# Recurrent stage of a fused decoder chain: bonus, gather, residual and statistics take other places in the step

## The chip, the cores and the metric

One core of a Trainium2 chip. The metric is the device time of one execution in microseconds: 3461.31 us before, the median of three runs (3460.58 to 3463.86). Below, TensorE is PE in the profile, VectorE DVE, ScalarE ACT, GpSimd POOL and SyncE SP.

## The reference, cut to what matters

Four layers follow one another on 16 sequences of 128 tokens with 512 features, in float32: masked self and cross attention with a feed-forward part (L0), grouped cross attention (L1), a recurrent block (L2) and a latent cross attention with a feed-forward part (L3). The change touches L2 alone:

```python
xa = _ln(x, ln1_w, ln1_b)
sx = concatenate([state[:, 1:2] - xa[:, :1], xa[:, :-1] - xa[:, 1:]], axis=1)
xxx = einsum(tanh((xa + sx * maa_x) @ maa_w1).reshape(b, l, 5, DM), maa_w2)
xm = xa[:, :, None] + sx[:, :, None] * (maa_stack + xxx)          # xk, xw, xv, xr, xg
w = exp(-exp(time_decay + tanh(xw @ td_w1) @ td_w2))
r, k, v, g = xr @ Wr.T, xk @ Wk.T, xv @ Wv.T, silu(xg @ Wg.T)
def step(s, (r_t, k_t, v_t, w_t)):
    a = k_t[..., :, None] * v_t[..., None, :]
    out = einsum('bhi,bhij->bhj', r_t, u * a + s)                  # u * a: the bonus
    return a + w_t[..., :, None] * s, out
og = head_norm(out) * gn_w + gn_b
x1 = x + og * g @ Wo.T
xc = _ln(x1, ln2_w, ln2_b)                                         # and a shift by one token again
return x1 + sigmoid(xr2 @ Wfr.T) * (square(relu(xk2 @ Wfk.T)) @ Wfv.T)
```

There are 32 heads of 16 x 16 states per sequence.

## The kernel before, in words

The program is a row of phases (self, cross, mlp, group, rec, latent, pmlp), with a barrier between two of them. The recurrent phase, `recurrence_phase` from L2159, handles one sequence per step and keeps five in flight. In step n the names stand for these sequences: `ahead` is n+1 (its rows are normalised, transposed and shifted), `front` n (low-rank mixes, decay, v, k, r, g), `middle` n-1 (the recurrence proper), `back` n-2 (head norm, output projection, residual, second norm, ffn keys and half of the receptance rows), `tail` n-3 (the rest of the ffn and the result). `run_steps` (L2142) runs steps -1 to 18, those in the middle in a loop of two steps.

Every engine has its own queue with a fixed order, written out by hand in its own `step` function: SyncE at L2352, GpSimd at L2408, ScalarE at L2566, VectorE at L2763, TensorE at L3042. Engines are tied together by semaphores alone. PSUM has five shared banks (`StepBanks`, L2096): the list at L2229 says in which order the items of a step use each bank, and TensorE's `begin` (L2858) waits for the use before to be free. Beside them, rec_out takes the head sums and two banks hold k.

The recurrence of a sequence is cut into 8 units (four feature chunks by two halves of the head). For unit u VectorE makes k times v (`inputs`, L2668, instruction L2674), then a scan over time (`scan`, L2678, L2686); GpSimd multiplies the states by r (`multiply_states`, L2382, L2386); TensorE sums over the head (`sum_heads`, L2981, L2987). Four buffers S circulate, whose first columns ScalarE copies (`first_states`).

The bonus is r times k on VectorE (`bonus_products`, L2690), a sum over the head weighted by u on TensorE (`bonus`, L2973), a copy to SBUF on ScalarE (`bonus`, L2539) and a product with v on GpSimd (`bonus_values`, L2390). `gather` (L2694) adds it to the head sums. Then comes the head norm: `mean` and `variance` on TensorE (L2991, L2999), `head_centre` and the Newton iterations of `head_rsqrt` on VectorE (L2699, L2704), `squares` and `affine` on ScalarE, `rstd_t` (L3007), `gated` (L2729). `out_rows` (L3012) projects; `residual` (L2735) adds the rows loaded again and takes mean and variance (`norm_stats`, L2625); `rsqrt` on GpSimd (L2375) makes the power -1/2 and its product with the negated mean; `normalise_back` and `shifted_back` on ScalarE (L2478, L2482) and `mix_back` on VectorE (L2745) feed the ffn. `stats_front` and `normalise_front` do the first norm for the sequence ahead.

The mixes (`mix`, L2645) come from TensorE in pairs (`mix_pair`, L2926); decay, v, k, r and g follow. `own_weights.wait` and `setup_done` guard weights and a few constants that VectorE prepares at the phase's start (L2828 to L2851).

## Time and profile before

| | us |
|---|---|
| median of three runs | 3461.31 |
| the profiled execution, its own time | 3457.59 |
| its span | 3455.8 |
| recurrent phase in the trace, about | 1571 to 2455 |

| engine | busy over the span | share |
|---|---|---|
| TensorE, matmul | 3175.1 us | 92% |
| VectorE | 1776.9 us | 51% |
| ScalarE | 1160.8 us | 34% |
| GpSimd | 793.3 us | 23% |

The shares are means over phases with different limits. In the page's slices VectorE is busy nine tenths only in the recurrent phase. A line of the timeline gives start, duration, engine, source line, operation and tiles, then in brackets the idle time just before it and what ended that idle. Neighbouring instructions of one kind are merged, and the printed ends of neighbours overlap by up to a tenth of a microsecond, so differences of starts are the better price.

### The profile page before, as it was taken

How to read it: one execution, taken by the hardware profiler on the slowest of the kernel's cores; microseconds unless marked ns; L12 is line 12 of the kernel's file. 1: busy time of each engine (PE TensorE's matmuls, PEld its weight loads, DVE VectorE, ACT ScalarE, POOL GpSimd, SP SyncE). 2: the span in 40 equal slices, each digit the busy share in tenths (PEclk: the TensorE clock that was granted, in tenths of full speed). 3: DMA queues.
4: the chain of work that ended last, by engine and by line, in shares of the span. 5: the costliest groups of instructions: out<-in, count | busy, mean ns of one | idle time of the engine just before them, and what ended most of it. 6: DMA issues, size and time to landing. Idle time of an engine off the chain costs nothing. (4 is left out here: it accounts for less than half of the span.)

```text
span 3455.8 us, 52394 instructions
## 1 busy us (share of the span) xinstructions
PE 3175.1 (92%) x19136; PEld 2078.5 (60%) x19136; DVE 1776.9 (51%) x2577; ACT 1160.8 (34%) x4083; POOL 793.3 (23%) x565
## 2 busy tenths in 40 slices
PE   7999899989999888886899999997799999899999
PEld 5666566657676655555666666664355555567675
DVE  4655455510000178874899999998254544400000
ACT  2444233421111266661333443342233333311111
POOL 2333233310000012222444444445000000100000
PEclk9999999989999999998899999998999999999999
DMA  4110231110000131112111111110130110101000
GB/s 166 42 46 27 80 131 52 40 64 22 15 21 17 42 150 47 49 39 68 35 51 38 37 49 37 41 43 28 64 133 26 36 41 20 49 22 33 21 33 12
DMA packets 104307, 170.17 MB, mean 49 GB/s; under 512 B 16512, under 2 KB 54016, under 8 KB 100736
## 3 DMA queue, kind: packets, MB, share of 16 engines
q1 hardware_dynamic: 99296, 124.58, 11.4%
q10 hardware_dynamic: 4896, 44.04, 3.1%
q8 instruction: 74, 1.21, 0.1%
q14 instruction: 41, 0.34, 0.0%
HBM read 135.03 MB, written 33.55 MB: 49 GB/s over the span
## 5 line engine op out<-in xcount | busy, mean ns | idle before, releaser
L2386 POOL TENSOR_TENSOR rec_S<-rec_S,rec_r_t 128x1024 f32<-128x1024 f32 x128 | 302.0, 2359 | 362.4 <-DVE rec_S L2686 362.3
L2686 DVE TENSOR_TENSOR_SCAN rec_S<-rec_decay,rec_S 128x1024 f32<-128x1024 f32 x128 | 318.0, 2484 | 5.8 <-ACT rec_S L2446 1.5
L2076 PE MATMUL mlp_bank<-mlp_src_t,region_a 128*128 128x256 f32 x1024 | 224.1, 382 | 3.1 <-ACT mlp_src_t L1997 3.1
L2076 PE MATMUL pmlp_bank<-pmlp_src_t,region_a 128*128 128x256 f32 x1024 | 224.7, 382 | 1.9 <-ACT pmlp_src_t L1997 1.9
L2088 PE MATMUL pmlp_bank<-region_a,pmlp_h_t 128*128 128x512 f32 x512 | 221.1, 593 | 0.0
L2088 PE MATMUL mlp_bank<-region_a,mlp_h_t 128*128 128x512 f32 x512 | 221.1, 593 | 0.0
L2076 PEld LDWEIGHTS mlp_bank<-mlp_src_t,region_a 128*128 128x128 f32 x1024 | 196.2, 192 | 32.9 <-issue 6.8
L2076 PEld LDWEIGHTS pmlp_bank<-pmlp_src_t,region_a 128*128 128x128 f32 x1024 | 196.6, 192 | 31.7 <-issue 5.5
L1505 ACT ACTIVATE group_scores<-group_scores,group_negmax 128x128 f32<-128x128 f32 x512 | 197.6, 392 | 28.4 <-DVE group_negmax L1599 18.5
L2043 DVE TENSOR_TENSOR mlp_y<-mlp_bank,mlp_xres 128x512 f32<-128x512 f32 x16 | 11.1, 692 | 374.2 <-PE mlp_bank L2088 374.2
L2043 DVE TENSOR_TENSOR pmlp_y<-pmlp_bank,pmlp_xres 128x512 f32<-128x512 f32 x16 | 11.1, 692 | 363.5 <-PE pmlp_bank L2088 363.5
L2006 ACT ACTIVATE pmlp_h_t<-pmlp_bank,vectors 128x256 f32<-128x256 f32 x128 | 53.7, 470 | 353.6 <-PE pmlp_bank L2076 353.6
L2006 ACT ACTIVATE mlp_h_t<-mlp_bank,vectors 128x256 f32<-128x256 f32 x128 | 53.6, 470 | 347.9 <-PE mlp_bank L2076 347.9
L2088 PEld LDWEIGHTS mlp_bank<-region_a,mlp_h_t 128*128 128x128 f32 x512 | 97.0, 191 | 118.4 <-issue 118.4
L2088 PEld LDWEIGHTS pmlp_bank<-region_a,pmlp_h_t 128*128 128x128 f32 x512 | 97.0, 190 | 118.4 <-issue 118.4
L2674 DVE TENSOR_TENSOR rec_S<-rec_vb,rec_k 128x1016 f32<-128x1016 f32 x128 | 154.0, 1203 | 0.0
L599 ACT ACTIVATE latent_scores<-latent_scores,region_a 128x256 f32<-128x256 f32 x256 | 126.4, 497 | 71.7 <-DVE region_a L789 71.7
L2987 PE MATMUL rec_rec_out<-rec_S,head_sum 128*32 128x256 f32 x1024 | 84.8, 404 | 45.8 <-POOL rec_S L2386 45.8
L973 PE MATMUL latent_pjA<-latent_src_t,F_query_key 128*128 128x512 f32 x256 | 122.0, 602 | 3.3 <-ACT latent_k_t L589 2.3
L599 ACT ACTIVATE self_scores<-self_scores,self_negmax 128x128 f32<-128x128 f32 x256 | 98.8, 390 | 77.0 <-DVE self_negmax L789 77.0
L599 ACT ACTIVATE cross_scores<-cross_scores,cross_negmax 128x128 f32<-128x128 f32 x256 | 98.7, 390 | 76.4 <-DVE cross_negmax L789 76.4
L1979 POOL TENSOR_TENSOR mlp_xres<-mlp_x,rows 128x512 f32<-128x512 f32 x16 | 20.2, 1264 | 341.0 <-DVE mlp_y L2043 329.6
(366 smaller groups left out, 6495.1 us busy)
## 6 DMA issues: line engine op xcount, KB each, us to landing
rec_vb<-v_by_head SPq DMA_DIRECT2D x32, 512.0 KB, 4.2
region_a<-in_C_w ACTq DMA_DIRECT2D x2, 4096.0 KB, 18.8
region_a<-in_G_w ACTq DMA_DIRECT2D x2, 4096.0 KB, 18.0
self_xres<-in_x SPq DMA_DIRECT2D x16, 256.0 KB, 2.6
rows_A<-self_xres SPq DMA_DIRECT2D x16, 256.0 KB, 2.0
cross_ctx_t<-in_ctx_t SPq DMA_DIRECT2D x16, 256.0 KB, 3.3
cross_xres<-rows_A SPq DMA_DIRECT2D x16, 256.0 KB, 2.6
rows_B<-cross_xres SPq DMA_DIRECT2D x16, 256.0 KB, 2.0
```

What stands on the lines that cost most here:

```text
L599: nc.scalar.activation(S[:, u, at, :], S[:, u, at, :], ACT.Exp, bias=negmax[:, u, at.start // KB:at.start // KB + 1], accum_out=rowsum[:, ...
L973: last = nc.tensor.matmul(pj.bank(item)[:, :], Wk[:, c, n * 128:n * 128 + 128], src_t[:, c, :, :], start=c == 0, stop=c == C - 1)
L1505: nc.scalar.activation(S[:, u, at, :], S[:, u, at, :], ACT.Exp, bias=negmax[:, u, at:at + 1], accum_out=rowsum[:, u // UPS, sum_column(u, ...
L1979: nc.gpsimd.tensor_tensor(xres[:, k, :], xr[:, k, :], row(cfg["b2"]), ALU.add)\
L2006: hidden = nc.scalar.activation(h_t[:, 2 * n + i, :], ph.bank(("h", n))[:, i * TT:(i + 1) * TT], ACT.Gelu_apprx_tanh, bias=vec(cfg["b1"], ...
L2043: nc.vector.tensor_tensor(y[:, k, :], po.bank(("out", k))[:, :], xres[:, k, :], ALU.add)\
L2076: product = nc.tensor.matmul(ph.bank(item)[:, i * TT:(i + 1) * TT], W1[:, c, f:f + 128], src_t[:, c, :, :], start=c == 0, stop=c == C - 1)
L2088: product = nc.tensor.matmul(po.bank(item)[:, :], h_t[:, c, k * T:k * T + T], W2[:, c, :], start=c == 0, stop=c == HC - 1)
L2386: nc.gpsimd.tensor_tensor(S[u % 4][:, :, :], S[u % 4][:, :, :], bcast(r_t[:, s.k, UNITS[u][0], :], [128, JH, T], 1), ALU.mult)\
L2674: nc.vector.tensor_tensor(S[u % 4][:, :, 1:T], vb[jh][:, :, 0:T - 1], bcast(k_bank[s.k][:, m * T:m * T + T - 1], [128, JH, T - 1], 1), ALU ...
L2686: nc.vector.tensor_tensor_scan(St[:, :, :].rearrange(flat), decay[m][:, :, :].rearrange(flat), St[:, :, :].rearrange(flat), 0.0, ALU.mult, ...
L2987: last = nc.tensor.matmul(rec_out[32 * g:32 * g + 32, jh * 2 * T:(jh + 1) * 2 * T], head_sum, S[u % 4][:, 2 * g:2 * g + 2, :], start=m == ...
```

## The change

It moves work to other places in the queues, and separates two buffers. The bonus product of `front` is made at the end of a step, where that of `middle` was made in its middle; the matmuls, the copy and the product with v follow early in the next step. The bonus's bank use moves from bank b to bank n. On VectorE the gather stands ahead of the first mix, the residual ahead of the output and of the inputs of unit 4, the front statistics ahead of unit 5. On TensorE one quarter of the receptance rows goes from the end of a step behind the low-rank product of the next, and the sum of unit 7 behind the low-rank transposes. On ScalarE the front normalisation goes ahead of the backward shifts. The negated mean is taken on GpSimd. x1 has two buffers, the normalised rows xn2 have their own (the squares of the head norm share it), so that of these only the tanh of the receptance waits for the store. In the first step TensorE and ScalarE no longer wait for constants and weights ahead of the first rows, but ahead of the low-rank product.

```diff
-        x1 = sb("x1", [128, D])
+        x1 = sb("x1", [128, SL, D])
-        y = xn2 = sb("y", [128, D])
+        xn2 = sb("xn2", [128, D])
+        sq = xn2[:, :].rearrange("p (c t) -> p c t", c=C)
+        y = sb("y", [128, D])
...
-            ("a", "mx", 0), ("a", "lt", 0), ("b", "mix1", 0), ("a", "mix2", 0), ("n", "mean", 2),
+            ("a", "mx", 0), ("a", "lt", 0), ("b", "mix1", 0), ("a", "mix2", 0), ("n", "c", 1), ("n", "mean", 2),
...
-            ("b", "c", 1), ("b", "x", -1), ("d", "fk", 2),
+            ("b", "x", -1), ("d", "fk", 2),
...
                 pool.wait_ge(var_done, n + 1)
+                nc.gpsimd.tensor_tensor(out[:, 2:3], tile[:, 6:7], minus_one[:, :], ALU.mult)
                 nc.gpsimd.tensor_tensor(out[:, 0:1], tile[:, 9:10], minus_half[:, 0:1], ALU.pow).then_inc(out_done, 1)
                 pool.wait_ge(out_done, n * 2 + 1)
-                nc.gpsimd.tensor_tensor(out[:, 1:2], tile[:, 8:9], out[:, 0:1], ALU.mult).then_inc(out_done, 1)
+                nc.gpsimd.tensor_tensor(out[:, 1:2], out[:, 2:3], out[:, 0:1], ALU.mult).then_inc(out_done, 1)
```

GpSimd's step:

```diff
                     first_columns(back)
                 if middle:
+                    bonus_values(middle)
                     multiply_states(middle, 2)
...
                     multiply_states(middle, 4)
-                if middle:
-                    multiply_states(middle, 5)
                 if ahead and not is_first(ahead.n):
                     rsqrt(ahead.n - 1, stats, rstd, front_norm[2], rstd_done)
                 if middle:
+                    multiply_states(middle, 5)
                     multiply_states(middle, 6)
-                    bonus_values(middle)
```

ScalarE (`rows_front`, `normalise_back`, `sigmoid_tanh` and the step):

```diff
+                if is_first(s.n):
+                    act.wait_ge(setup_done, SETUP)
...
-                wait_count(act, stored, s.n * 16)
-                normalise(s.n, xn2, x1, rstd2, rstd2_done, xn2_done)
+                normalise(s.n, xn2, x1[:, s.k, :], rstd2, rstd2_done, xn2_done)
...
                 full(act, s, "fr")
+                wait_count(act, stored, s.n * 16)
...
                     low_rank_copy(front)
+                if middle:
+                    bonus(middle)
                 if middle:
                     make_decay(middle, 3)
...
                     receptance(front)
+                if ahead and not is_first(ahead.n):
+                    normalise_front(ahead)
                 if back:
                     shifted_back(back)
...
                     make_decay(front, 0)
-                if ahead and not is_first(ahead.n):
-                    normalise_front(ahead)
-                if front:
                     gate(front)
-                if middle:
-                    bonus(middle)
...
-            act.wait_ge(setup_done, SETUP)
             run_steps(act, step)
```

VectorE:

```diff
-                nc.vector.tensor_scalar(tile[:, 8:9], tile[:, 6:7], -1.0, None, ALU.mult)
...
             def bonus_products(s):
                 freed(dve, s, "r")
+                dve.wait_ge(k_full, s.n + 1)
...
-                if not is_first(s.n):
-                    freed(dve, Before(s), "fv")
+                if not (isinstance(s.n, int) and s.n < 2):
+                    freed(dve, Before(s, 2), "fv")
...
                     scan(middle, 0)
+                if back:
+                    gather(back)
                 if front:
                     mix(front, 1)
-                if back:
-                    gather(back)
...
                     mix(front, 3)
+                if back:
+                    residual(back)
                 if tail:
                     output(tail)
                 if middle:
                     inputs(middle, 4)
-                if back:
-                    residual(back)
-                if middle:
                     scan(middle, 4)
                 if front:
                     mix(front, 4)
+                if ahead and not is_first(ahead.n):
+                    stats_front(ahead)
                 if middle:
                     inputs(middle, 5)
                     scan(middle, 5)
-                    bonus_products(middle)
-                if ahead and not is_first(ahead.n):
-                    stats_front(ahead)
-                if middle:
                     inputs(middle, 6)
...
                     shift_front(ahead)
+                if front:
+                    bonus_products(front)
```

TensorE:

```diff
-            own_weights.wait(pe)
-
...
             def low_rank(s):
+                if is_first(s.n):
+                    own_weights.wait(pe)
+                    pe.wait_ge(setup_done, SETUP)
...
                     low_rank(front)
+                if tail:
+                    ffn_gate(tail, 1)
+                if front:
+                    low_rank_t(front)
                 if back:
                     sum_heads(back, NU - 1)
-                if front:
-                    low_rank_t(front)
                 if tail:
                     ffn_gate(tail, 2)
                 if front:
                     mix_pair(front, 1, 2)
+                if middle:
+                    bonus(middle)
...
                     sum_heads(middle, 5)
-                    bonus(middle)
...
-                    ffn_gate(back, 0, 1)
+                    ffn_gate(back, 0)
...
-            pe.wait_ge(setup_done, SETUP)
             run_steps(pe, step)
```

## Rows read from the trace of the kernel before

**Rows 1.** Windows, one steady step: busy (count) PE, PEld, DVE, ACT, POOL; PEclk; DMA; GB/s.

```profile
1961.40:2012.00 50.60, 46.19 (x358) 33.68 (x357) 47.84 (x67) 19.42 (x49) 23.96 (x16) 1.00 0.13 42
```

**Rows 2.** Timeline of VectorE, one steady step from shift to shift.

```profile
1961.43 0.66 DVE L2642 TENSOR_TENSOR rec_sx_t<-rec_xa_t,rec_bank_b 128x512 f32<-128x512 f32 x1
...
1967.10 0.70 DVE L2652 TENSOR_TENSOR rec_bank_b<-rec_bank_b,rec_sx_t 128x512 f32<-128x512 f32 x1 [1.01 <-PE rec_bank_b L2913]
...
2009.01 3.06 DVE L2686 TENSOR_TENSOR_SCAN rec_S<-rec_decay,rec_S 128x1024 f32<-128x1024 f32 x1
...
2012.00 0.66 DVE L2642 TENSOR_TENSOR rec_sx_t<-rec_xa_t,rec_bank_b 128x512 f32<-128x512 f32 x1
```

**Rows 3.** Timeline of VectorE, the same step, units 4 and 5 and around.

```profile
1987.14 0.70 DVE L2652 TENSOR_TENSOR rec_bank_b<-rec_bank_b,rec_sx_t 128x512 f32<-128x512 f32 x1 [0.20 <-PE rec_bank_b L2913]
...
1988.48 0.69 DVE L2758 SCALAR_TENSOR_TENSOR rec_bank_d<-rec_y,rec_bank_d 128x512 f32<-128x512 f32 x1
...
1990.93 0.69 DVE L2740 TENSOR_TENSOR rec_x<-rec_bank_c,rec_xr 128x512 f32<-128x512 f32 x1
...
1992.65 0.15 DVE L2633 TENSOR_SCALAR rec_stats<-rec_stats 128x1 f32<-128x1 f32 x1
...
1992.82 2.29 DVE L2686 TENSOR_TENSOR_SCAN rec_S<-rec_decay,rec_S 128x1024 f32<-128x1024 f32 x1
...
1996.35 1.20 DVE L2674 TENSOR_TENSOR rec_S<-rec_vb,rec_k 128x1016 f32<-128x1016 f32 x1
...
1997.58 2.60 DVE L2686 TENSOR_TENSOR_SCAN rec_S<-rec_decay,rec_S 128x1024 f32<-128x1024 f32 x1
...
2000.68 0.68 DVE L2628 BATCH_NORM_STATS2 rec_stats<-rec_x 128x6 f32<-128x512 f32 x1
...
2001.81 1.20 DVE L2674 TENSOR_TENSOR rec_S<-rec_vb,rec_k 128x1016 f32<-128x1016 f32 x1
```

**Rows 4.** Timeline of GpSimd, the same step.

```profile
1992.95 2.50 POOL L2378 TENSOR_TENSOR rec_rstd<-rec_stats,minus_half 128x1 f32<-128x1 f32 x1 [3.58 <-DVE rec_stats L2634]
...
2002.58 0.55 POOL L2378 TENSOR_TENSOR rec_rstd<-rec_stats,minus_half 128x1 f32<-128x1 f32 x1
...
2008.65 1.27 POOL L2393 TENSOR_TENSOR rec_bv<-rec_v_t,rec_c_sb 128x512 f32<-128x512 f32 x1
```

**Rows 5.** Timeline of TensorE, the same step.

```profile
1969.18 1.16 PE L2995 MATMUL rec_bank_n<-rec_og,region_a 128*128 128x128 f32 x8 [1.05 <-DVE rec_og L2697]
...
1979.53 3.84 PE L2874 MATMUL rec_bank_b<-rec_xm,region_a 128*128 128x128 f32 x32 [0.96 <-ACT rec_e_t L2514]
...
1987.04 1.99 PE L2880 MATMUL rec_bank_c<-region_a,rec_og_t 128*128 128x512 f32 x4
...
1988.86 1.95 PE L2874 MATMUL rec_k<-rec_xm,region_a 128*128 128x128 f32 x16
...
1998.09 0.64 PE L2987 MATMUL rec_rec_out<-rec_S,head_sum 128*32 128x256 f32 x8 [1.16 <-POOL rec_S L2386]
...
2003.39 1.16 PE L2977 MATMUL rec_bank_b<-rec_rk,region_a 128*128 128x128 f32 x8
...
2004.93 0.66 PE L2867 MATMUL rec_bank_b<-ident,rec_x 128*128 128x128 f32 x4 [0.38 <-ACT rec_c_sb L2542]
```

**Rows 6.** Timeline of SyncE's queue, the same step: both loads of v.

```profile
1995.95 13.79 SPq L2349 DMA_DIRECT2D rec_vb<-v_by_head  x2
```

**Rows 7.** Timelines of TensorE and ScalarE at the phase's start; DMA issues there.

```profile
1574.16 1.09 PE L2867 MATMUL rec_bank_b<-ident,first_x 128*128 128x128 f32 x4 [12.13 <-DVE rec_touched L2851]
...
1575.28 1.50 ACT L2463 ACTIVATE rec_xa_t<-rec_bank_b,vectors 128x128 f32<-128x128 f32 x4 [1.15 <-PE rec_bank_b L2867]
...
1576.84 2.50 PE L2898 MATMUL rec_bank_a<-region_a,rec_xa_t 128*128 128x160 f32 x8 [1.59 <-ACT rec_xa_t L2463]
...
rec_st<-in_state_t SPq DMA_DIRECT2D x3, 2.0 KB, 1.8
```

**Rows 8.** Timeline of VectorE, the last step with states: scan of unit 5.

```profile
2396.49 3.91 DVE L2686 TENSOR_TENSOR_SCAN rec_S<-rec_decay,rec_S 128x1024 f32<-128x1024 f32 x1
```

More of the change, by code:

```diff
@@ L2187, in recurrence_phase @@
         stats = sb("stats", [128, 10])
-        rstd = sb("rstd", [128, 2])
+        rstd = sb("rstd", [128, 3])
+        minus_one = sb("minus_one", [128, 1])
         touched = sb("touched", [128, 1])
@@ L2249, in recurrence_phase @@
         zero_done = sem("zero_done")
+        one_done = sem("one_done")
         front_norm = (sem("stat_done"), sem("aggr_done"), sem("var_done"))
@@ L2429, in step @@
                 if middle:
+                    multiply_states(middle, 5)
                     multiply_states(middle, 6)
-                    bonus_values(middle)
+            nc.gpsimd.memset(minus_one[:, :], -1.0).then_inc(one_done, 1)
+            pool.wait_ge(one_done, 1)
             pool.wait_ge(setup_done, SETUP)
@@ L2737, in residual @@
                 dve.wait_ge(xr_loaded, s.n * 16 + 16)
-                if not is_first(s.n):
-                    freed(dve, Before(s), "fv")
-                nc.vector.tensor_tensor(x1[:, :], banks.bank("o")[:, :], xr[:, :], ALU.add)\
+                if not (isinstance(s.n, int) and s.n < 2):
+                    freed(dve, Before(s, 2), "fv")
+                nc.vector.tensor_tensor(x1[:, s.k, :], banks.bank("o")[:, :], xr[:, :], ALU.add)\
                     .then_inc(banks.free_sem("o"), 1)
                 freed(dve, s, "o")
-                norm_stats(s.n, x1, stats2, touched2, back_norm)
+                norm_stats(s.n, x1[:, s.k, :], stats2, touched2, back_norm)
             def mix_back(s, q):
@@ L2759, in output @@
                 dve.wait_ge(u_done, s.n + 1)
-                nc.vector.scalar_tensor_tensor(y[:, :], product, 0.5, x1[:, :], ALU.mult, ALU.add)\
+                nc.vector.scalar_tensor_tensor(y[:, :], product, 0.5, x1[:, s.k, :], ALU.mult, ALU.add)\
                     .then_inc(banks.free_sem("fv"), 1)
```

3 lines of the change are left out of this document (1 added, 2 removed).

## The prediction

> **What bounds the kernel now.** I read the busy tenths of the page first. Seven phases follow one another, and the change touches only the recurrent one, about 1571 to 2455 us; the rest keeps its time. I then cut that phase into windows of one step (one sequence per step, sixteen sequences, five stages in flight). In a steady step [rows 1] TensorE works 46.2 us of 50.6 and VectorE 47.8, at a granted clock of 1.00: two engines at over nine tenths, which hand work to each other many times a step. The waits must decide. The step repeats exactly: the shift starts at 1961.43 and again at 2012.00, 50.6 us later [rows 2].
>
> VectorE's timeline shows three kinds of loss. It idles 1.01 us before the first mix, for TensorE [rows 2], and 0.20 before the fourth [rows 3]; and some scans are long: 3.06 and 2.60 us, where the plain one takes 2.29 [rows 2, 3]. GpSimd's timeline says why [rows 4]: the bonus multiply holds from 2008.65 to 2009.92, and the scan issued at 2009.01 ends 2.15 after that. Conversely the small power of the norm, 0.55 alone, takes 2.50 when issued inside a scan. So a scan and a GpSimd multiply exclude each other, while mixes and statistics run beside them at their usual length. TensorE waits four times that matter [rows 5]: 1.16 for the product of state 4, 0.96 for the decay exponent ahead of v, 0.38 for the bonus copy before the next rows' transposes; and 1.05 ahead of the mean, for the gather that stands behind the first mix.
>
> **Part by part, one steady step.** Starts are subtracted, so that overlaps are in.
> - The negated mean leaves VectorE twice: under 0.15 each (L2633 in [rows 3]), about 0.07 as they overlap. GpSimd gets one more tiny operation per norm, about 0.15, before the power, beside VectorE's work.
> - Bonus: same work (VectorE 0.5 to 0.6, between the end of scan 5 at 2000.18 and the statistics at 2000.68; TensorE 1.16; GpSimd 1.27 [rows 3 to 5]). Its product goes behind the shift of the rows ahead, its matmuls behind the first pair of mixes, its copy ahead of the last decay, its GpSimd multiply ahead of state 2. Gone: the 0.78 by which it held scan 7, and the 0.38 before the transposes. Not free: 1.0 of TensorE now stands ahead of the mean.
> - ScalarE's queue: the bonus copy now waits there for the first mixes' and the bonus matmuls, about 2 us, with the last decay (about 1) behind it; that is needed only at scan 3, over 10 us later, so nothing. The front rows' normalisation (0.8) goes ahead of the eight shifts (2.9); they end about 9.4 after scan 4 starts, the backward mix is ready for them at 9.1: 0.3 of idle on VectorE. On GpSimd the bonus multiply fits between states 1 and 2, while VectorE runs the head norm: nothing, and 1.27 on the product of state 2 if it came late.
> - One quarter of the receptance rows (about 1.0, half of a 1.99 group [rows 5] being one quarter) goes behind the low-rank product, in the place where TensorE now waits for the last state's product, whose sum goes behind the low-rank transposes.
> - Gather ahead of the first mix: that mix's 1.01 idle is filled by the gather's 0.60, and mean starts earlier as seen from scan 0.
> - Residual ahead of the output and of the inputs of state 4: its statistics end 2.6 before scan 4 instead of at its start, so the power no longer falls inside a scan; GpSimd takes state 4 at once and scan 5 loses its 0.3. But out-rows ends about 0.5 after the fourth mix is done, and VectorE will now idle for that.
> - Front statistics ahead of scan 5: 1.13, now 1.06 [rows 3], moves onto the way from scan 4 to scan 5. That delays the product of state 5, which TensorE needs after the gate projection.
> - Two x1 buffers, xn2 apart from y, and the wait for the store moved to the tanh: costless, as the store awaited was issued a step's larger part before. What would be late next is the load of v: in SyncE's queue the store, which waits for the output, stands ahead of the writes and loads of v. The output moves 1.7 nearer to scan 4 (the residual's 1.82 changes sides), so the first load, issued at 1995.95 [rows 6] would be there by 2002 if it takes the page's 4.2 to land, ten before its first use behind the shift at 2012.00. Nothing is charged; with that cover gone each 1 us late would be 1 us.
>
> With these orders the closed chain of a step is no longer VectorE alone. **TensorE's part** runs from the head sum of state 5 to the end of out-rows. It is all its work, 46.2, less what lies from keys to that sum: 1988.86 to 2003.39, less the sum 0.57 and the wait 1.16, is 12.8. That leaves 33.4. Behind it stay the wait for the exponent, 0.96, and an estimated 0.3 for the gated output. By this sum 34.7; by adding the starts of each block, which leaves out tails that overlap, 34.1. **VectorE's and GpSimd's part** leads back [rows 3]: residual 1.82 (1.89 less 0.07), output and inputs 4 to the next start 2.45, 0.1 more for the scan's semaphore, scan 4 and the fifth mix 3.53, statistics 1.06, inputs 5 1.23, scan 5 2.29 and 0.08 to GpSimd's start, product 2.36, 0.05 for the semaphore (the sum at 1998.09 starts that much behind its release): 15.0. **The step comes to 49.1 to 49.7; I take 49.3, 1.3 less than 50.6.** VectorE's own work in it is about 46.2, so it idles some 3: before the centre (mean is late by about 0.6), before the variance 0.4, at out-rows 0.5, at the fourth mix 0.3, at the first backward mix 0.3.
>
> Twelve steps are full and two more nearly so (one without a tail, one without rows ahead): 14 x 1.3 = 18.2.
>
> **The start** [rows 7]. TensorE transposes the first rows at 1574.16, released by VectorE's last constant, ScalarE's four activations take 1.50 from 1575.28, and the low-rank product follows at 1576.84. The transposes need no constant; the product does. The state column's load is issued with the phase at about 1571 and lands after 1.8, so ScalarE can copy at 1572.9 and finish by 1574.5; the constants are there since 1574.1. Gain 2.3. Below: 0, if the load lands 2.3 later than its median; above 2.7, no more than TensorE's present distance from constants to product.
>
> **First filled step and drain.** In the first step with states a norm operation caught in a scan costs about what the 2.50 row shows, 1.9 over its own 0.55; TensorE, at a lower clock there, then gates most of it, and I keep 1, between 0 and 2. In the last one scan 5 takes 3.91, held by a state 4 that started late [rows 8]: 1.5 back, against the bonus matmuls ahead of the mean, up to 2 at twice their 1.0: I keep 1 with the last bonus multiply out of the way (1.27), between -1 and 3.
>
> Sum: 18.2 + 2.3 + 1 + 1 = 22.5 us. The profiled execution took 3457.6 around a span of 3455.8; it becomes 3435.1. The median of the three runs is 3461.3, 3.7 higher, so I give 3438.8. Its own bounds: 0.6 a step with 4 around it, 12 us, 3449; and 2.2 a step (half of the 4.4 between 50.6 and VectorE's own 46.2) with 7 around it, 38 us, 3423.
>
> **One rule weighed.** In the new order three small GpSimd operations of the front norm stand between state 4's product and scan 5. From scan 4's start: product over at 4.73 (2.29, 0.08, 2.36), variance ready at about 4.66 (3.53 and 1.13), the last small operation issued at about 5.5 (0.15 for the new one, 0.62 for the power and its semaphore [rows 4]), scan 5 at 5.8 (3.53, 1.06, 1.23): a margin of 0.3. What the loser pays is in the power's row: 2.50 against 0.55. That is the third rival. The Trainium skill (SBUF — State Buffer, section SBUF: two separate sides) says that a VectorE instruction with two SBUF inputs and a GpSimd one that reads SBUF contend for one port pair, an exclusive lock held by whoever starts first for the whole instruction. By that rule the trace agrees to 0.15 us: a scan held up ends 2.15 after the multiply, not 2.29. My sum has no held scan left in a steady step, so it is the same by either.
>
> **Rivals.**
> 1. TensorE swallows it. Bonus and the receptance quarter ahead of the mean make the centre, and all behind it, late by more than the 0.6 I count, and nothing of the waits comes back but the 0.3 and 0.4 around scans. For it: TensorE at 46.2. Against: it also starts its step 2.0 sooner. A step gains 0 to 0.5: 4 to 11 us in all, 3450 to 3457.
> 2. VectorE stays the bound and all waits go: a step of about 47.5, 3.1 less; with 4 around it, 47 us: 3414. Against it: TensorE's waits at state 5 and at the exponent remain.
> 3. Slower: the front norm's last operation misses scan 5. It waits out the scan, the normalised rows come 2.5 late, ScalarE's eight shifts stand behind them on its queue, the backward mix slips by 2.5, and state 6's product with it; TensorE arrives at its sum 2.4 later. Step 51.7, 1.1 over now: 14 x 1.1 less 4.3 = +11: 3472. It decides if GpSimd is 0.3 us later against scan 5 than I add up.
> 4. The moves gain nothing and only the start is real: 3459.
>
> **Chances.** My forecast, 3423 to 3449: 0.68. Rival 1: 0.14, two thirds of it still beyond 0.2%. Rival 2 below 3423: 0.08. Rival 3: 0.07. Rival 4: 0.03. 0.2% is 7 us, about what a measurement of this kernel tells from no change. Faster by more: 0.85; within: 0.08 (a third of rival 1, and rival 4); slower: 0.07. The range takes the forecast's bounds and most of rival 1: 3423 to 3453.
>
> **What would show it.** Right: steady steps of 49.3; no scan over 2.4 but perhaps scan 0; no power over 0.6; a TensorE wait of about 1 before the sum of state 5 and none for the bonus copy; VectorE idle before the centre and before the residual, about 0.5 each; transposes near 1571. Wrong: power or its multiply near 2.5 us with an idle of 2 or more before the backward mix (rival 3), an idle before the centre over 1.5 (rival 1), steps under 48 (rival 2).

## The result and the profile after

The changed kernel takes 3442.7 us (median of 5 runs, 3441.6 to 3447.6) against 3461.3 (5 runs, 3460.2 to 3463.9): ratio 0.9948, 95% interval 0.9935 to 0.9961. It is 18.6 us faster; 22.5 were forecast. The profiled execution took 3441.6 around a span of 3439.8.

The windows view of one steady step, from shift to shift, answers to [rows 1]:

```profile
2002.10:2051.30 49.20, 45.61 (x358) 33.55 (x357) 46.45 (x64) 19.19 (x51) 22.37 (x18) 1.00 0.13 43
```

VectorE is busy for 1.4 us less in it, mostly since the three long scans of a step, whose wait counted as busy, are gone. Its timeline in that step answers to [rows 2, 3]:

```profile
2002.08 0.66 DVE L2647 TENSOR_TENSOR rec_sx_t<-rec_xa_t,rec_bank_b 128x512 f32<-128x512 f32 x1
...
2007.63 0.70 DVE L2657 TENSOR_TENSOR rec_bank_b<-rec_bank_b,rec_sx_t 128x512 f32<-128x512 f32 x1 [0.17 <-PE rec_bank_b L2919]
...
2010.38 0.69 DVE L2707 TENSOR_TENSOR rec_og<-rec_og,rec_bank_n 128x512 f32<-128x512 f32 x1 [0.22 <-PE rec_bank_n L3001]
...
2014.89 0.19 DVE L2714 TENSOR_SCALAR rec_hv<-rec_bank_n 128x32 f32<-128x32 f32 x1 [0.30 <-PE rec_bank_n L3009]
...
2027.14 0.70 DVE L2657 TENSOR_TENSOR rec_bank_b<-rec_bank_b,rec_sx_t 128x512 f32<-128x512 f32 x1 [0.20 <-PE rec_bank_b L2919]
...
2029.07 0.69 DVE L2746 TENSOR_TENSOR rec_x<-rec_bank_c,rec_xr 128x512 f32<-128x512 f32 x1 [0.43 <-PE rec_bank_c L2883]
...
2033.57 2.29 DVE L2691 TENSOR_TENSOR_SCAN rec_S<-rec_decay,rec_S 128x1024 f32<-128x1024 f32 x1
...
2039.48 2.29 DVE L2691 TENSOR_TENSOR_SCAN rec_S<-rec_decay,rec_S 128x1024 f32<-128x1024 f32 x1
...
2049.13 2.29 DVE L2691 TENSOR_TENSOR_SCAN rec_S<-rec_decay,rec_S 128x1024 f32<-128x1024 f32 x1
2051.34 0.66 DVE L2647 TENSOR_TENSOR rec_sx_t<-rec_xa_t,rec_bank_b 128x512 f32<-128x512 f32 x1
```

The step is 49.26 here and 49.51 the next time; the two alternate, and the mean is 49.37. The idle before the first mix fell from 1.01 to 0.17; new, small ones stand before the centre and the residual. Those before the variance and the fourth mix are as they were: the kernel before has 0.30 and 0.20 there. The last scan, 3.06 before, is plain. So is the first scan of the step, which the prediction names only as a "perhaps". Two lines of the kernel before, then the first scan now:

```profile
1963.34 2.75 DVE L2686 TENSOR_TENSOR_SCAN rec_S<-rec_decay,rec_S 128x1024 f32<-128x1024 f32 x1
...
1974.88 0.19 DVE L2708 TENSOR_SCALAR rec_hv<-rec_bank_n 128x32 f32<-128x32 f32 x1 [0.30 <-PE rec_bank_n L3003]
```

```profile
2004.58 2.29 DVE L2691 TENSOR_TENSOR_SCAN rec_S<-rec_decay,rec_S 128x1024 f32<-128x1024 f32 x1
```

It was held by 0.46 behind the last state's product; the bonus product on VectorE, which now stands ahead of it, fills that time.

GpSimd's timeline shows the front norm's three small operations (the first is new here, the second is the power of [rows 4]) and the next product:

```profile
2038.39 0.19 POOL L2382 TENSOR_TENSOR rec_rstd<-rec_stats,rec_minus_one 128x1 f32<-128x1 f32 x1
2038.53 0.54 POOL L2383 TENSOR_TENSOR rec_rstd<-rec_stats,minus_half 128x1 f32<-128x1 f32 x1
2039.14 0.19 POOL L2385 TENSOR_TENSOR rec_rstd<-rec_rstd 128x1 f32<-128x1 f32 x1
2041.85 2.36 POOL L2391 TENSOR_TENSOR rec_S<-rec_S,rec_r_t 128x1024 f32<-128x1024 f32 x1 [2.51 <-DVE rec_S L2691]
```

The last of them starts at 2039.14, scan 5 at 2039.48: 0.34 ahead. TensorE's timeline has these waits. Of those in [rows 5] two are gone, the one before the mean and the one before the transposes of the next rows:

```profile
1995.01 0.64 PE L2993 MATMUL rec_rec_out<-rec_S,head_sum 128*32 128x256 f32 x8 [1.13 <-POOL rec_S L2391]
...
2019.54 3.84 PE L2877 MATMUL rec_bank_b<-rec_xm,region_a 128*128 128x128 f32 x32 [0.96 <-ACT rec_e_t L2521]
...
2038.35 0.64 PE L2993 MATMUL rec_rec_out<-rec_S,head_sum 128*32 128x256 f32 x8 [1.41 <-POOL rec_S L2391]
...
2044.27 0.64 PE L2993 MATMUL rec_rec_out<-rec_S,head_sum 128*32 128x256 f32 x8 [1.12 <-POOL rec_S L2391]
```

The closed chain can be read off: from the sum of state 5 (1995.01) to the residual (2029.07) 34.06, and on to the next sum of state 5 (2044.27) 15.20; together 49.26, the step (they must add up to it, since both ends are the same sum; what is measured is how it divides).

Cut by starts on VectorE (first memset of the phase, the sixteen shifts, first memset of the next phase), the phase of the profiled executions divides so, all kernels of this study in one table:

```
us                   start+step 0  step 1  step 2  12 steps  each    rest    phase
before                  40.47      45.36   51.43   607.6    50.63   142.09   886.95
after                   41.06      43.52   49.40   592.4    49.37   143.70   870.08
e1_start_only           40.35      45.35   51.44   607.6    50.63   142.10   886.81
e2_gather_back          40.77      43.53   51.98   599.2    49.93   144.66   880.13
e3_residual_back        37.99      43.53   51.18   611.9    50.99   139.71   884.28
e4_stats_back           37.65      44.86   47.92   640.1    53.34   143.91   914.39
e5_bonus_back           38.01      44.77   49.29   599.3    49.94   146.02   877.41
e6_quarter_back         41.00      43.53   51.92   595.3    49.61   142.15   873.87
e7_late_norm            40.26      43.54   51.81   622.9    51.91   141.74   900.27
e8_output_first         40.53      43.52   51.52   579.8    48.32   140.54   855.92
e9_output_second        40.54      43.53   51.51   583.8    48.65   140.25   859.59
e10_stats_back_two      38.01      44.70   47.79   592.8    49.40   143.78   867.06
e11_filled_start        35.58      42.32   49.44   579.9    48.32   139.60   846.79
e12_filled_drain        37.18      40.92   51.39   579.8    48.32   136.56   845.89
```

Each row is one profiled execution. After less before: start and step 0 +0.6, step 1 -1.8, step 2 -2.0, twelve steps -15.2, rest +1.6: -16.9. The start, from which 2.3 was expected, gave nothing.

### The profile page after: what moved, and what is told of

It is laid out like the page before. It is cut to its first block and busy times, and to the rows that moved or that the text cites. A ratio compares the mean times of both kernels' runs of the same rounds, so it can differ in the third digit from the quotient of the medians.

```text
span 3439.8 us, 52480 instructions
## 1 busy us (share of the span) xinstructions
PE 3167.9 (92%) x19136; PEld 2074.6 (60%) x19136; DVE 1759.4 (51%) x2546; ACT 1158.5 (34%) x4083; POOL 766.1 (22%) x597
## 5 line engine op out<-in xcount | busy, mean ns | idle before, releaser
L2691 DVE TENSOR_TENSOR_SCAN rec_S<-rec_decay,rec_S 128x1024 f32<-128x1024 f32 x128 | 298.5, 2332 | 4.7
L1505 ACT ACTIVATION_READ_ACCUMULATOR group_scores<-group_scores,group_negmax 128x1 f32 x512 | 98.0, 191 | 0.0
## 6 DMA issues: line engine op xcount, KB each, us to landing
region_a<-in_C_w ACTq DMA_DIRECT2D x2, 4096.0 KB, 18.7
```

The source lines that it names most:

```text
L1505: nc.scalar.activation(S[:, u, at, :], S[:, u, at, :], ACT.Exp, bias=negmax[:, u, at:at + 1], accum_out=rowsum[:, u // UPS, sum_column(u, ...
L2691: nc.vector.tensor_tensor_scan(St[:, :, :].rearrange(flat), decay[m][:, :, :].rearrange(flat), St[:, :, :].rearrange(flat), 0.0, ALU.mult, ...
```

## The experiments

**The parts of the steady step, undone one at a time.** Each of the next four kernels is the changed one with one part put back. First the gather:

```diff
-                if back:
-                    gather(back)
                 if front:
                     mix(front, 1)
+                if back:
+                    gather(back)
```

> The changed kernel with the gather behind the first mix again. Theory (closed chain): the first mix waits for TensorE as now, the gather ends 0.4 after the place where TensorE is ready for the mean, so the centre and the step slip by 0.4: steps of 49.8, +6 us on the changed kernel, 3449. Rival (the gather filled a whole idle of 1.0): steps of 50.4, +14 us, 3457.

Measured 3452.4 us, ratio to the kernel before 0.9981 (0.9971 to 0.9990). A step takes 49.93, 0.57 more than in the changed kernel. The theory's 0.4 is nearer than the rival's 1.0.

The quarter of the receptance rows, and with it the place of the last head sum:

```diff
                 if front:
                     low_rank(front)
-                if tail:
-                    ffn_gate(tail, 1)
+                if back:
+                    sum_heads(back, NU - 1)
                 if front:
                     low_rank_t(front)
-                if back:
-                    sum_heads(back, NU - 1)
...
                 if back:
-                    ffn_gate(back, 0)
+                    ffn_gate(back, 0, 1)
```

> The changed kernel with two quarters of the receptance rows at the end of a step and the last head sum ahead of the low-rank transposes, as before. Theory: the sum waits for its product 0.3, the first mixes and the mean come 0.3 later: steps of 49.7, +4 us, 3447. Rival (the quarter was worth its whole length): steps of 50.3, +13 us.

Measured 3446.3 us, 0.9955 (0.9941 to 0.9969). A step takes 49.61, 0.24 more, as the theory had it. Two moves were undone together, so the 0.24 is not the quarter's alone.

The bonus: its products back between scan 5 and the inputs of state 6, its matmuls ahead of the rows' transposes, its copy behind the decay and the gate, its GpSimd multiply behind state 6.

```diff
                     scan(middle, 5)
+                    bonus_products(middle)
                     inputs(middle, 6)
...
                     shift_front(ahead)
-                if front:
-                    bonus_products(front)
```

> The changed kernel with the whole bonus where it was. Theory: the GpSimd multiply holds scan 7 by 0.8 again and the transposes wait 0.4 for the copy, against 1.0 less of TensorE ahead of the mean: steps 49.7 to 50.2, +4 to +11 us, and the first filled step loses most of its 1.8. Rival (the bonus ahead of the mean costs what it brings): steps of 49.4 or less, 0 or below.

Measured 3449.2 us, 0.9966 (0.9954 to 0.9979). A step takes 49.94, 0.58 more, inside the theory's band, and step 1 takes 1.25 more. In its steady steps the last scan takes about 3.07 again and the first about 2.76.

The residual:

```diff
-                if back:
-                    residual(back)
                 if tail:
                     output(tail)
                 if middle:
                     inputs(middle, 4)
+                if back:
+                    residual(back)
+                if middle:
                     scan(middle, 4)
```

> The changed kernel with output and inputs 4 ahead of the residual again. Theory (what the move buys is the norm outside a scan): scan 4 starts 0.7 earlier, but the power is caught in it, state 4 starts 0.7 after its end instead of 0.1, its product ends 38.2 where scan 5 starts at 38.7, and the three small operations of the front norm (0.95) miss scan 5: backward mix late by about 2, steps of 50.7 to 51.2, +18 to +25 us. Rival (the residual's place matters by its idle alone): steps 48.7 to 49.4, -9 to 0 us.

Measured 3458.9 us, 1.0001 (0.9991 to 1.0011): without this part the change brings nothing. A step takes 50.99, 1.62 more, inside the theory's band and 0.36 over the kernel before. GpSimd's timeline in a steady step of it; scan 4 starts at 2042.00 and scan 5 at 2047.92:

```profile
2042.07 2.21 POOL L2382 TENSOR_TENSOR rec_rstd<-rec_stats,rec_minus_one 128x1 f32<-128x1 f32 x1 [3.58 <-DVE rec_stats L2639]
...
2045.00 2.36 POOL L2391 TENSOR_TENSOR rec_S<-rec_S,rec_r_t 128x1024 f32<-128x1024 f32 x1
...
2048.07 2.12 POOL L2385 TENSOR_TENSOR rec_rstd<-rec_rstd 128x1 f32<-128x1 f32 x1
```

An operation on one element a partition is caught in scan 4 and takes 2.21. State 4's product starts behind it, 3.00 after the scan's start, where the changed kernel has 2.37: 0.6 late. So the front norm's operations are late too, and the last is caught in scan 5 by 0.15.

**The race itself.** This kernel leaves the order alone and puts four tiny multiplications of a spare tile, 0.63 us, on GpSimd ahead of the front norm's operations, more than the 0.34 by which the last one leads scan 5.

```diff
                 if ahead and not is_first(ahead.n):
+                    pool.wait_ge(front_norm[2], ahead.n)
+                    for i in range(4):
+                        nc.gpsimd.tensor_tensor(spare[:, i:i + 1], minus_one[:, :], minus_one[:, :], ALU.mult)
                     rsqrt(ahead.n - 1, stats, rstd, front_norm[2], rstd_done)
```

> The changed kernel with four more tiny GpSimd operations (about 0.14 each, 0.56 together, on a tile nobody reads) between the front variance and the front norm. The trace gives a margin of 0.34 between the last small operation and scan 5. Theory (third rival of the forecast, the port): the last operation misses scan 5 and waits it out, the backward mix comes about 2 late, steps of 51.5, +30 us, 3473. Rival (only the 0.56 counts): steps of 49.4 to 50.0, 0 to +8 us.

Measured 3475.7 us, 1.0043 (1.0026 to 1.0059). A step takes 51.91, 2.54 more for 0.63 of work. Its GpSimd timeline, the four spare operations first, then VectorE's:

```profile
2005.85 0.63 POOL L2435 TENSOR_TENSOR rec_spare<-rec_minus_one 128x1 f32<-128x1 f32 x4
...
2006.57 0.54 POOL L2384 TENSOR_TENSOR rec_rstd<-rec_stats,minus_half 128x1 f32<-128x1 f32 x1
2007.19 2.04 POOL L2386 TENSOR_TENSOR rec_rstd<-rec_rstd 128x1 f32<-128x1 f32 x1
```

```profile
2006.94 2.29 DVE L2695 TENSOR_TENSOR_SCAN rec_S<-rec_decay,rec_S 128x1024 f32<-128x1024 f32 x1
...
2012.88 1.12 DVE L2760 SCALAR_TENSOR_TENSOR rec_f_in<-rec_bank_c,rec_w_same,rec_f_in 128x128 f32<-128x128 f32 x4 [2.55 <-ACT rec_f_in L2500]
```

The last operation comes 0.25 behind the scan's start and ends with it; the normalised rows, the shifts and the backward mix are 2.5 late. This is what the prediction's third rival described: it priced the step at 51.7 and the whole at 3472.

**The statistics.** Here the front statistics go behind scan 5 again, with their GpSimd operations and the normalisation on ScalarE. VectorE's part of the edit:

```diff
-                if ahead and not is_first(ahead.n):
-                    stats_front(ahead)
                 if middle:
                     inputs(middle, 5)
                     scan(middle, 5)
+                if ahead and not is_first(ahead.n):
+                    stats_front(ahead)
+                if middle:
                     inputs(middle, 6)
```

> The changed kernel with the front statistics behind scan 5 again, the front norm's three small GpSimd operations behind state 5, and the front normalisation behind the shifts, as before. My sum charges 1.06 of the closed chain to the statistics ahead of scan 5. Counting from scan 4: state 5 ends 9.5, the last small operation is issued at 10.2, scan 6 at 10.2: a tie. Theory (the norm follows): if it wins, TensorE waits for the next rows instead of for state 5, steps of 49.3 to 49.6, 0 to +4 us; if it loses, the rows come 2 later and steps are 51 to 51.5, +20 to +30 us. Rival (the statistics' place alone costs 1.06): steps of 48.3, -14 us.

Measured 3486.9 us, 1.0076 (1.0057 to 1.0096): slower than either kernel. A step takes 53.34, 4 more than in the changed kernel, and more than either branch allowed. GpSimd's timeline, then the wait that follows on TensorE; scan 6 starts at 2007.92:

```profile
2007.34 0.54 POOL L2383 TENSOR_TENSOR rec_rstd<-rec_stats,minus_half 128x1 f32<-128x1 f32 x1
2007.95 2.24 POOL L2385 TENSOR_TENSOR rec_rstd<-rec_rstd 128x1 f32<-128x1 f32 x1
```

```profile
2011.17 0.65 PE L2873 MATMUL rec_bank_b<-ident,rec_x 128*128 128x128 f32 x4 [3.25 <-ACT rec_x L2481]
```

The operation missed the scan by 0.03 us. Was that the whole of it, or does so late a place cost 4 us by itself? The same kernel, with the negated mean on VectorE as in the kernel before, answers:

```diff
-                nc.gpsimd.tensor_tensor(out[:, 2:3], tile[:, 6:7], minus_one[:, :], ALU.mult)
...
+                nc.vector.tensor_scalar(tile[:, 8:9], tile[:, 6:7], -1.0, None, ALU.mult)
```

> e4 (front statistics, the norm's small operations and its normalisation behind scan 5) with the negated mean back on VectorE, so that GpSimd has two small operations before its last one instead of three. In e4 the last one was issued 0.03 us after scan 6 had started, and waited for it: steps of 53.3. Taking one away brings the last one about 0.14 earlier and VectorE's extra operation puts scan 6 about 0.07 later, so it now starts 0.15 to 0.2 ahead of the scan. Theory (the step is decided by which of the two takes the port first): every last operation is back to about 0.2 us, nothing waits for the rows over 1 us, steps of 49.3 to 50.3, total 3440 to 3457. Rival (the late place of the statistics itself costs the 4 us, by the queue of ScalarE and TensorE's rows): steps stay at 52.5 to 53.5, total 3475 to 3490.

Measured 3442.7 us, 0.9952 (0.9936 to 0.9969), with steps of 49.40: the time of the changed kernel, 44 us below e4. GpSimd's timeline; scan 6 starts at 2043.42, 0.17 behind the second line:

```profile
2042.63 0.54 POOL L2382 TENSOR_TENSOR rec_rstd<-rec_stats,minus_half 128x1 f32<-128x1 f32 x1
2043.25 0.19 POOL L2384 TENSOR_TENSOR rec_rstd<-rec_stats,rec_rstd 128x1 f32<-128x1 f32 x1
```

So with the norm behind scan 5 the negated mean on GpSimd costs 4 us a step. Ahead of scan 5 no run has it on VectorE, so what its move is worth there is not shown. The two moves together, as the changed kernel has them, gain no time on e10 (49.37 against 49.40), but a margin of 0.34 in place of 0.17.

**The output.** VectorE's part of the chain, 15.2, holds the output, 1.34, which the chain has no need of there. These two kernels take it out, e8 and e9 in this order:

```diff
+                if tail:
+                    output(tail)
                 if front:
                     mix(front, 3)
                 if back:
                     residual(back)
-                if tail:
-                    output(tail)
```

> The changed kernel with the output (1.33 on VectorE) between scan 3 and the fourth mix. Theory (VectorE's chain from out-rows back to the sum of state 5 is part of the closed chain): the idles of 0.20 before the fourth mix and 0.43 before the residual are filled, scan 4 comes 0.6 earlier: steps of 48.8, -9 us, 3434. Rival (TensorE bounds the step): its waits at states 4 and 5 shrink or move and the step stays at 49.3.

```diff
                 if front:
                     mix(front, 3)
+                if tail:
+                    output(tail)
                 if back:
                     residual(back)
-                if tail:
-                    output(tail)
```

> The changed kernel with the output between the fourth mix and the residual, instead of behind the residual. e8, with the output ahead of the fourth mix, took 1.05 us off each step; two things moved there at once. Theory (the 0.43 us of idle before the residual, which waits for out-rows, is what counts; the output covers it, and the state 4 chain only needs VectorE's sum of work): the wait before the residual goes, the fourth mix keeps its 0.20, steps of 48.4 to 48.6, total near 3428 to 3432. Rival (what counts is the place of the fourth mix, which TensorE and ScalarE need for the gate, and its covered wait): steps of 48.9 to 49.2, 3437 to 3441. Third possibility, no gain at all, since the residual's statistics are only moved later against scan 4 and a power is caught in it: a GpSimd operation of over 2 us in each step and 51, as in e3.

Measured 3426.5 us, 0.9896 (0.9879 to 0.9912), and 3430.4, 0.9917 (0.9900 to 0.9933); steps of 48.32 and 48.65. VectorE's timeline of e8, then TensorE's:

```profile
2025.12 0.67 DVE L2764 SCALAR_TENSOR_TENSOR rec_bank_d<-rec_y,rec_bank_d 128x512 f32<-128x512 f32 x1
...
2026.43 0.69 DVE L2657 TENSOR_TENSOR rec_bank_b<-rec_bank_b,rec_sx_t 128x512 f32<-128x512 f32 x1
...
2027.83 0.68 DVE L2746 TENSOR_TENSOR rec_x<-rec_bank_c,rec_xr 128x512 f32<-128x512 f32 x1
```

```profile
2035.66 0.64 PE L2993 MATMUL rec_rec_out<-rec_S,head_sum 128*32 128x256 f32 x8 [0.47 <-POOL rec_S L2391]
...
2041.59 0.64 PE L2993 MATMUL rec_rec_out<-rec_S,head_sum 128*32 128x256 f32 x8 [1.13 <-POOL rec_S L2391]
```

The waits before the fourth mix and the residual are gone, residual to sum is 13.76 in place of 15.20, and TensorE's wait for state 4 shrinks from 1.41 to 0.47. In e9 the fourth mix keeps its 0.20, the residual's wait is gone, and TensorE's wait is 0.77. The rival of e8, that TensorE bounds the step, is refuted. But e8 gained 1.05 a step where its theory had 0.6, so that theory was too small; e9's 48.65 lies 0.05 outside its own band, far from both its rivals. Part of the difference can be read off: by starts, scan 3 to scan 4 takes 8.91 in the changed kernel, 8.27 in e9 and 7.97 in e8, which is 0.64 and 0.94 less, and more than the printed waits of 0.43 and of both, 0.63. The remaining 0.1 goes with the alternation of 49.26 and 49.51, which e8 does not have.

**The start.** The kernel before with the start alone changed:

```diff
 in low_rank, TensorE:
+                if is_first(s.n):
+                    own_weights.wait(pe)
+                    pe.wait_ge(setup_done, SETUP)
 ahead of the steps, TensorE:
-            own_weights.wait(pe)
-            pe.wait_ge(setup_done, SETUP)
```

> The kernel before with the start's waits moved and nothing else. My forecast gave this 2.3 us; the trace of the changed kernel shows the first low-rank product 2.0 earlier after the phase's first instruction, and its first step ending 0.6 later all the same, at a granted clock of 0.70 against 0.82. Theory (the clock takes it back): product 2.0 earlier, first shift after it not earlier by more than 0.5, total 3461 +- 1.5. Rival (the loss in the first step belongs to other moves, such as the bonus product behind the shift): first shift of step 1 2 us earlier, total about 3459.

Measured 3458.9 us, 1.0000 (0.9990 to 1.0009). The interval is 3 us wide to either side, so the medians cannot tell 2.3 us from nothing; the pieces can. The low-rank product stands 4.1 after the phase's start, 1.8 sooner than before, and start and step 0 take 40.35 against 40.47: nothing, though the rows do start sooner. It is so in the changed kernel too. Its timelines of TensorE and ScalarE answer to [rows 7], and its phase begins at 1571.8, 0.8 later:

```profile
1571.74 1.09 PE L2870 MATMUL rec_bank_b<-ident,first_x 128*128 128x128 f32 x4 [8.88 <-PEq L189]
1575.61 2.47 PE L2904 MATMUL rec_bank_a<-region_a,rec_xa_t 128*128 128x160 f32 x8 [2.79 <-ACT rec_xa_t L2469]
```

```profile
1573.87 0.20 ACT L2466 COPY rec_xa_t<-rec_st 128x4 f32<-128x4 f32 x1 [19.71 <-DMA rec_st<-in_state_t]
1573.97 1.50 ACT L2469 ACTIVATE rec_xa_t<-rec_bank_b,vectors 128x128 f32<-128x128 f32 x4
```

The low-rank product stands 3.8 after the phase's start, 5.9 before: 2.0 sooner. Behind it the clock takes it back. The stretch of 4 us from 1580 was granted 0.93 in the kernel before; here, in the changed kernel (the same columns as [rows 1]), the granted clock is 0.50, its lower level of 1.2 GHz, until past 1592:

```profile
1580.00:1584.00 4.00, 2.67 (x18) 2.02 (x19) 0.00 (x0) 0.89 (x4) 0.00 (x0) 0.50 0.01 2
1584.00:1588.00 4.00, 2.50 (x14) 1.80 (x11) 2.69 (x4) 0.00 (x0) 0.00 (x0) 0.50 0.00 0
1588.00:1592.00 4.00, 2.42 (x17) 2.16 (x18) 1.39 (x2) 1.41 (x5) 0.00 (x0) 0.50 0.00 0
1592.00:1596.00 4.00, 4.00 (x23) 4.00 (x22) 0.00 (x1) 0.00 (x0) 0.00 (x0) 0.57 0.02 4
```

The same start ran in nine kernels derived from the changed one. In the profiled executions its time goes with the clock granted in the first 24 us of the phase:

```
                                granted, first 24 us    start and step 0
e3, e4, e5, e10                     0.71 to 0.72          37.7 to 38.0
e2, e6, e7                          0.57 to 0.59          40.3 to 41.0
e8, e9, the changed kernel          0.51 to 0.52          40.5 to 41.1
the kernel before                   0.66                  40.5
```

The four fastest are 2.5 to 2.8 us under the kernel before, whose clock was nearly theirs: near the 2.3 forecast. To give TensorE work in the gaps, e11 adds spare transposes to e8, into a bank not yet in use.

```diff
+            def filler(n):
+                for _ in range(n):
+                    nc.tensor.transpose(rec_out[:, 0:128], ident, ident)
 ...
                     transpose(s, "x", first_rows.x[:, 0, :])
+                    filler(6)
```

> e8 with spare transposes of the identity into a bank that nothing reads yet, in the gaps of TensorE's first step alone: six behind the transposes of the first rows, one behind the low-rank product, two behind its transposes, three behind each first pair of mixes. They are work added. Theory (the start gains nothing because TensorE, mostly waiting there, stays at the lower clock for five windows of 4 us): with the gaps filled the granted clock reaches 1.00 earlier than at 1592, and start plus step 0 takes 38 to 39.5 us instead of 40.5; total about 1 to 2.5 us under e8, which only the phase's pieces can show. Rival (the chain of small operations sets the start, not the clock): start plus step 0 stays at 40.3 to 41.5, whatever the clock does; total as e8, or up to 1 us more. Steady steps 48.3 in both.

Measured 3420.7 us, 0.9888 (0.9871 to 0.9905). Windows of its start:

```profile
1580.00:1584.00 4.00, 2.99 (x22) 2.52 (x23) 0.00 (x0) 0.89 (x4) 0.00 (x0) 0.87 0.41 156
1584.00:1588.00 4.00, 2.55 (x29) 1.98 (x28) 2.69 (x4) 0.27 (x1) 0.00 (x0) 1.00 0.00 0
1588.00:1592.00 4.00, 2.81 (x33) 2.62 (x30) 1.39 (x2) 1.14 (x4) 0.00 (x0) 1.00 0.02 4
1592.00:1596.00 4.00, 3.31 (x36) 3.00 (x36) 0.23 (x1) 0.60 (x1) 0.00 (x0) 1.00 0.01 3
```

The clock is at its upper level, 2.4 GHz, from 1584 on, and start and step 0 take 35.6 where e8 has 40.5: 5 us for added work, twice what the theory dared. In e12 below, with the same start, they take 37.2; over the first 24 us the clock was 0.86 and 0.79 in the two. Beside the best start without filler, 37.7, the gain is 2.1 and 0.5. How much of it reaches the medians is not shown: e11's ratio is 0.0008 (3 us) under e8's, well inside both intervals, and e8's profiled execution is the slowest of its four (3430.4). The Trainium skill (TensorE: Matmul & The Clock Gate, section Part 1: The HAM clock gate) says that the lower clock is the default and that activity releases it. By that rule the trace agrees: the stretch of 4 us from 1588 was granted 0.50 in e8 without the filler, 1.00 in e11 and e12 with it.

**The drain.** e12 adds the same to TensorE's gaps in the last two steps, 103 transposes in seven places, of which this is one:

```diff
+                if drain:
+                    drain_filler(14)
                 if back:
                     out_rows(back, 0, 1)
```

> e11 with spare transposes of the identity in TensorE's gaps of the drain too (the last step with states and the one behind it, 103 of them, into a bank that is no longer used): 8 ahead of the last sum of the sequence before, 14 ahead of each out-rows, 28 and 14 ahead of the transposes of the normed rows, 9 and 16 ahead of the keys. In e11 TensorE waits 2.5 to 7.3 us at these places, the clock falls to 0.50 behind them, and out-rows takes 3.75 and 5.24 us, the keys 5.73 and 5.16 where a steady step has 1.96 for half of out-rows and 3.8 for the keys. Theory (my term for the drain failed for want of the clock: TensorE at the lower level makes VectorE wait for the mean, the residual and the backward mix): clock 1.00 through the drain, and the drain, 139.6 in e11, takes 133.5 to 137; total 3 to 6 us under e11. Rival (the drain is the chain of scans and products, which no clock touches): keys and out-rows get shorter, but the drain stays at 139 to 140.5, total as e11.

Measured 3420.8 us, 0.9886 (0.9869 to 0.9904). The rest of the phase takes 136.6 where e11 has 139.6, inside the theory's band. TensorE's timeline of e11, then of e12, with the out-rows of the last sequence and their wait:

```profile
2390.22 5.24 PE L2883 MATMUL rec_bank_c<-region_a,rec_og_t 128*128 128x512 f32 x8 [3.24 <-DVE rec_og_t L2738]
```

```profile
2390.42 3.67 PE L2883 MATMUL rec_bank_c<-region_a,rec_og_t 128*128 128x512 f32 x8 [1.71 <-DVE rec_og_t L2738]
```

But the clock was not held everywhere (the keys still take 5.43 and 5.44, where e11 has 5.73 and 5.16), and the total is e11's: in this execution start to step 2 took 2.2 more than in e11, with the same code. That the drain's 3 us reach the median is therefore not shown.

## Why the prediction was right, and where it was off

- **Steady step: right.** 49.3 forecast, 49.37 measured, and by the chain given: TensorE's part 34.1 to 34.7, measured 34.06; the other 15.0, measured 15.20. The twelve full steps gave 15.2, the one without a tail 2.0 and the one without rows ahead 1.4 (scan 0 to scan 0 of the next step, 49.59 before, 48.17 after). That is 18.7, where 18.2 was forecast.
- **Its parts.** Undone singly they cost 0.57 (gather), 0.24 (quarter), 0.58 (bonus), 1.62 (residual) and 4.0 (statistics; 0.03 with one GpSimd operation less, in e10): far more than 1.27 together. They are not terms to be added: e3 and e4 show that a part put back can also lose the race for a scan. The bonus was priced with one held scan, the last (0.78); it held the first too, by 0.46, which e5 brings back.
- **Waits.** On VectorE, the fourth mix 0.3 forecast, 0.20 measured; the residual 0.5 and 0.43; the variance 0.4 and 0.30; the centre 0.6 and 0.22; the backward mix 0.3 and about 0.1. On TensorE, the wait for state 5 about 1, measured 1.12. A wait of 1.41 for state 4 (1.16 before) was not forecast; with the output's 1.34 moved away e8 has 0.47 there.
- **The third rival** was priced well: margin 0.3, measured 0.34; step 51.7, in e7 51.91. Beside it e4 shows that a miss can cost 4 when the norm stands still later: there TensorE itself waits 3.25 for the rows.
- **Held operations.** The Trainium skill (SBUF — State Buffer, section SBUF: two separate sides) makes the port pair a lock that the first to start keeps. The runs agree down to the smallest operation: 0.19 us alone, and 2.04 (e7), 2.12 and 2.21 (e3) and 2.24 (e4) when issued inside a scan.
- **First filled step:** +1 forecast between 0 and 2, measured 1.8, in part by luck. The norm's operation was caught there before (2.12) and is not now (0.19), as the term said. But in e5 it is not caught either, and the step is only 0.6 under the kernel before; the other 1.25 goes with the bonus's place, for which the term had nothing.
- **The start: mis-sized**, 2.3 forecast between 0 and 2.7, -0.6 measured. The product did come 2.0 sooner. The step that failed is silent: that the work behind keeps its length. It runs at a clock that differs from one profiled execution to the next, 0.66 before and 0.51 after over the first 24 us, and 2.6 us were taken back. Where the clock stayed near that of before (e3, e4, e5, e10) the term came out at 2.5 to 2.8.
- **The drain: mis-sized**, +1 forecast between -1 and 3, about -3.0 measured beside the fourteenth step, outside the term's own bounds. The last filled step's scan 5 was still held, 3.43 in place of 3.91, so 0.5 of the 1.5 came back. The last bonus multiply out of the way gave 0.9 of its 1.27. What failed is again silent: that the residual's new place costs as little in the drain as in a steady step. There out-rows take 3.75 for their first half at the lower clock, in both kernels, and the residual, with the output and the inputs of state 4 now behind it, waits for them. VectorE's timeline, before and after:

```profile
2391.21 0.69 DVE L2740 TENSOR_TENSOR rec_x<-rec_bank_c,rec_xr 128x512 f32<-128x512 f32 x1 [0.73 <-PE rec_bank_c L2880]
```

```profile
2372.51 0.69 DVE L2746 TENSOR_TENSOR rec_x<-rec_bank_c,rec_xr 128x512 f32<-128x512 f32 x1 [2.69 <-PE rec_bank_c L2883]
```

  Scan 3 to scan 4 takes 9.92 there, 7.88 before, 2.0 of the 3.0. In e3, with the residual behind the inputs again, it is 7.31; in e6 and e7, whose scans 0 to 3 keep e3's distances to 0.01, it is 9.51 and 9.55. The last sequence alone adds 1.5, with out-rows of 6.27 (5.37 before) at the lower clock. The clock has its own part: e12 changes only TensorE's gaps and brings 3.0 back in its one profiled execution.
- **Sum.** 18.7 + 1.8 - 0.6 - 3.0 = 16.9 for the phase in the profiled executions; the medians give 18.6. The steps carry the forecast of 22.5; start and drain were 3.3 promised and 3.6 lost.

## What to carry to other kernels

Find the chain that closes on itself, one engine's part and the others', and take out of it what only happens to stand there: the output's two instructions, moved ahead, gained 16 us more, nearly as much as the whole change. Where two engines share a port with an instruction of 2.3 us, a neighbour of 0.2 us has to start ahead of it with a margin: 0.03 behind or 0.17 ahead made 44 us of the total. Price a move again at the pipeline's end, where matmuls take longer and a new place can mean a new wait. And look at the granted clock there: idle gaps of TensorE filled with spare transposes shortened the start by 5 us beside the same kernel without them, in single profiled executions, which the medians do not confirm.

## What the runs showed of the hardware

A GpSimd operation on one element a partition, issued inside a scan, waits out the scan (0.19 us becomes 2.04 to 2.24). The granted clock at the phase's start comes out differently for the same start. In the changed kernel it stays at 0.50 to past 1592; in e10 it rises early, and falls back once. Windows of e10, whose phase begins 2.7 later:

```profile
1582.00:1586.00 4.00, 1.74 (x20) 1.28 (x19) 0.88 (x2) 0.89 (x4) 0.00 (x0) 1.00 0.03 6
1586.00:1590.00 4.00, 2.99 (x24) 2.55 (x24) 1.80 (x3) 0.27 (x1) 0.00 (x0) 0.78 0.00 0
1590.00:1594.00 4.00, 2.83 (x15) 2.77 (x14) 1.39 (x2) 1.14 (x4) 0.00 (x0) 0.50 0.01 4
```

Start and step 0 take 38.0 in it, 41.1 in the changed kernel. What decides this without filler was not tried and is open: each kernel has one profiled execution, so it may differ from run to run. In all, the medians of e11 and e12 are 38 and 40 us under the kernel before, each beside its own runs of it, and 22 under the changed one.
